# Four column tiles of 32 in place of two of 64, in the paired panels of a graph layer

## What is computed

```python
h = relu(layernorm(x))
u = par_u[0] * par_u[1] * (diag_u[:, None] * h[:2048] @ W_u) + h[:2048]
i = par_i[0] * par_i[1] * (diag_i[:, None] * h[2048:] @ W_i) + h[2048:]
e = concatenate([u, i])
h2 = adj @ (adj.T @ e)
out = x + layernorm(h2) * ln_gamma + ln_beta + h
```

## Time and profile before

| | us |
|---|---|
| median of 3 runs | 376.25 |
| lowest and highest | 376.2, 376.77 |
| span of the profiled execution | 374.4 |
| PE busy | 367.1 |
| DVE busy | 251.5 |
| ACT busy | 73.5 |
| POOL busy | 23.7 |

### The profile page before, as it was taken

One profiled execution on the slowest core, in us unless ns is written; L12 is line 12 of the kernel. 1 busy time (PEld: TensorE's weight loads), 2 busy tenths in 40 slices (PEclk: granted clock), 3 DMA queues, 4 the chain that ended last, 5 costly groups with the idle time before them and its releaser, 6 DMA issues.

```text
span 374.4 us, 8614 instructions
## 1 busy us (share of the span) xinstructions
PE 367.1 (98%) x3768; PEld 152.5 (41%) x3768; DVE 251.5 (67%) x249; ACT 73.5 (20%) x214; POOL 23.7 (6%) x30
## 2 busy tenths in 40 slices
PE   7999999999999999999999999999999999999995
PEld 5764455543334333433333343334333335436432
DVE  5999995859344965595289349754963793382366
ACT  4863012100032004000400320031004002202322
POOL 2023060000000000000000000000000000000036
PEclk9999999999999999999999999999999999999998
DMA  8999999999999999799969987997999699929603
GB/s 310 421 417 414 422 421 420 422 418 361 417 424 421 353 417 424 273 358 414 426 269 360 429 364 258 398 429 279 356 428 424 256 354 345 425 95 399 270 0 141
DMA packets 19896, 133.22 MB, mean 356 GB/s; under 512 B 2208, under 2 KB 2976, under 8 KB 4000
## 3 DMA queue, kind: packets, MB, share of 16 engines
q1 hardware_dynamic: 19440, 132.22, 87.4%
q10 hardware_dynamic: 432, 0.66, 0.5%
HBM read 131.55 MB, written 1.31 MB: 355 GB/s over the span
## 4 chain that ended last, share of the span: by engine, by line
PE 87%; DMA 7%; POOL 2%; SPq 2%; DVE 1%; issue 0%; ACT 0%; DVEq 0%; POOLq 0%
PE h_acc L756 35%; PE t_acc L782 32%; PE t_acc L725 10%; PE h_acc L739 9%; DMA natural<-adj_rows 7%; SPq L239 1%; POOL xs L360 1%; POOL scaled L356 1%; PE t_acc L800 1%; DVE xs L663 0%; SPq L236 0%; DVE scaled L652 0%; DVE natural L639 0%; PE h_acc L819 0%; DVE var L493 0%
## 5 line engine op out<-in xcount | busy, mean ns | idle before, releaser
L530 DVE STREAM_TRANSPOSE strips<-natural 128x2048 f32<-128x2048 f32 x76 | 168.2, 2274 | 48.4 <-PE h_acc L756 48.4
L756 PE MATMUL h_acc<-strips,centred 32*64 32x512 f32 x2432 | 133.3, 589 | 0.0
L782 PE MATMUL t_acc<-natural,e 128*64 128x512 f32 x560 | 121.4, 592 | 0.0
L756 PEld LDWEIGHTS h_acc<-strips,centred 32*64 32x64 f32 x2432 | 52.8, 132 | 78.5 <-issue 78.5
L782 PEld LDWEIGHTS t_acc<-natural,e 128*64 128x64 f32 x560 | 40.2, 137 | 79.9 <-issue 79.9
L725 PE MATMUL t_acc<-natural,e 128*64 128x256 f32 x480 | 54.1, 381 | 0.7 <-DMA natural<-adj_rows 0.6
L403 ACT COPY t_high<-t_acc 64x256 f32<-64x256 f32 x20 | 7.4, 368 | 212.6 <-PE t_acc L782 173.2
L539 DVE TENSOR_TENSOR t_sum<-t_acc,t_high 64x256 f32<-64x256 f32 x20 | 8.2, 410 | 57.0 <-ACT t_high L403 57.0
L725 PEld LDWEIGHTS t_acc<-natural,e 128*64 128x64 f32 x480 | 33.8, 137 | 20.6 <-issue 3.0
L410 ACT COPY centred<-centred 32x384 f32<-32x384 f32 (+2 forms) x60 | 24.2, 403 | 66.2 <-DVE centred L552 65.7
L739 PE MATMUL h_acc<-cols,centred 128*64 128x512 f32 x160 | 37.1, 599 | 0.0
(11 more groups left out here) (55 smaller groups left out, 86.6 us busy)
## 6 DMA issues: line engine op xcount, KB each, us to landing
natural<-adj_rows SPq DMA_DIRECT2D x100, 1024.0 KB, 11.8
cols<-adj_cols SPq DMA_DIRECT2D x20, 1024.0 KB, 7.6
natural<-adj_last SPq DMA_DIRECT2D x4, 1024.0 KB, 11.2
out<-xs SPq DMA_DIRECT2D x4, 256.0 KB, 2.0
xs<-x ACTq DMA_DIRECT2D x2, 256.0 KB, 5.4
xs<-x SPq DMA_DIRECT2D x2, 256.0 KB, 8.3
out<-xs SPq DMA_DIRECT2D x2, 128.0 KB, 2.0
smalls<-small SPq DMA_DIRECT2D x1, 150.0 KB, 3.3
```

The lines of the kernel that those rows point to most:

```text
L530: nc.vector.transpose(strips[:, a, :, m].rearrange("p c t i -> p t c i"), natural[:, a, m].rearrange("p t (c j) -> p t c j", j=Q)).then_in ...
L756: last = nc.tensor.matmul(h_acc[D * s:D * (s + 1), q], t[part, a, b, u, :], rows, start=(isinstance(g, int) and g == 0 and b == 0 and u == 0),
L782: last = nc.tensor.matmul(t_acc[D * s:D * (s + 1), c].rearrange("p (a w) -> p a w", a=2), e[:, GT * m + 2 * k + s, :], natural[:, :, m, HA ...
```

## The change

In `first_pair` each matmul of 64 stationary columns becomes two of 32, into PSUM partitions 0, 32, 64 and 96. The moving operand of the two with the same s is the same. `second_pair` calls a new function for the loaded columns that does the same there. Strips, single panels, the loaded columns of single panels, transfers and the work of the other engines stay as they are.

```diff
                     for k in range(HALF):
-                        for s in range(2):
-                            last = nc.tensor.matmul(t_acc[D * s:D * (s + 1), c].rearrange("p (a w) -> p a w", a=2),
-                                                    e[:, GT * m + 2 * k + s, :], natural[:, :, m, HALF * s + k],
+                        for s, v in itertools.product(range(2), range(D // Q)):
+                            lane = D * s + Q * v
+                            last = nc.tensor.matmul(t_acc[lane:lane + Q, c].rearrange("p (a w) -> p a w", a=2),
+                                                    e[:, GT * m + 2 * k + s, Q * v:Q * (v + 1)],
+                                                    natural[:, :, m, HALF * s + k],
                                                     start=(m == 0 and k == 0),
                                                     stop=(m == GROUPS - 1 and k == HALF - 1))
                     last.then_inc(s_first, 2)
+
+            def second_loaded_quarters(g, a, half):
+
+                pe.wait_ge(s_cols[a], 16 * (half + 1))
+                pe.wait_ge(s_t, g + 1)
+                for b in range(BLOCKS):
+                    for s, v in itertools.product(range(2), range(D // Q)):
+                        lane = D * s + Q * v
+                        last = nc.tensor.matmul(h_acc[lane:lane + Q, LOADED], t[:, a, b, 0, Q * v:Q * (v + 1)],
+                                                cols[:, a, s, b], start=False, stop=False, skip_group_check=True)
+                last.then_inc(s_loaded_done, 1)
 
             def second_pair(g, half):
                 for a in range(2):
                     second_strips(g + a, a).then_inc(s_strips_done, 1)
                 for a in range(2):
-                    second_loaded(g + a, a, half)
+                    second_loaded_quarters(g + a, a, half)
```

## The result

| | before | after |
|---|---|---|
| median of the runs, us | 376.23 | 399.81 |
| lowest and highest | 376.11, 376.77 | 399.61, 401.4 |
| ratio | | 1.0626 (1.0604 to 1.0647) |
| span of the profiled execution | 374.4 | 397.7 |

The direction and the place were foreseen, the size was not: 23.6 us where 4.9 was forecast, and the time lies above the range (376.3 to 388.0).

What follows compares the result with a forecast made beforehand. PE was taken to bound the kernel alone, any wait of PE adding in full. Borders with stagger +0.5 us and two jumps back +4.4 us on 376.25 gave 381.1 us, range 376.3 to 388.0.

Steps and rivals of the forecast that it cites:

- The rounds: Product 1 and loaded columns of the pairs: 336 rounds before and after, four column tiles running together, cost 0.
- Weight loads: They double in number, but four lie well inside a 0.43 us round, hidden by running matmuls.
- The borders: Three new ones where 128 x 32 meets 128 x 64, 0.15 us each; with the stagger +0.5 us (0 to 0.7).
- The stagger: Two further tiles add 13 ns at a round's start, paid at 14 borders at most where four-tile stages end: 0.2 us.
- That the loop's code no longer fits: PE's loop grows from 5.4 to 6.9 packets, one more ahead; code is refetched at the jumps back, chance 0.56.
- The price of a jump: Each of two jumps back waits for one packet: 4.7 - 2.5 = 2.2 us, together 4.4 us (0 to 11.0).
- The fetch: One instruction packet at a jump back takes 4.7 us, between bounds of 2.0 and 7.6.
- the lead of the sequencer: At the branch 20 to 29 matmuls are still queued on PE, hiding 2.5 us of the fetch (2.1 to 3.1).
- Later packets of the turn are asked for ahead and stay hidden.: After a jump back, only the first packet makes PE wait; later ones come as in the first turn, without cost.
- The wait is simply added.: While PE stands still at a jump, transfers and DVE go on, so nothing is late behind it.
- That the code still fits: Rival for PE's loop: jumps cost nothing, only +0.5 us remains, 376.7 us (376.25 to 377.0); chance 0.32.
- that four tiles don't run together: Rival for the rounds: they take twice their time, 520 us, or loads lose their cover, 423 us; chance 0.09.

Runs made afterwards that it cites:

- the moved loop of 1757 instructions: Changed kernel with four column tiles in product 1 only (loaded columns keep two), plus 52 waits (26 instructions) ahead of the loop: 378.42 us, ratio 1.0056.
- of 1501 instructions: Changed kernel with four column tiles in the loaded columns of the pairs only, product 1 keeping two of 64: 377.32 us, ratio 1.0022.
- the moved one: Whole change with 52 waits (26 instructions) ahead of the loop, so its first instruction begins a block of code: 389.4 us, ratio 1.0365.

## Why the prediction failed in size

**The rounds** were right. Four column tiles run together: product 1 is 160 matmuls in 17.17 us, to the hundredth what 80 took before. Nothing was won and nothing lost.

**Weight loads** were right: with twice as many of them product 1 takes the same 17.17 us, so they stay hidden.

**The borders** were right. Forecast +0.5 (0 to 0.7), measured 0.35 in the pairs. The price of a border where only the width changes, which no row of before showed, is 0.15 us (17.32 less 17.17), as taken; the three new ones are 0.14 (24.17 less 24.03), 0.15 (7.06 less 6.91) and 0.15 (10.51 less 10.36). The stagger, put at up to 0.2 us, didn't show: the loaded columns take 3.57 us where they took 3.58. That the loaded columns are quartered along with product 1 saves seven such borders, which the kernel with four tiles in product 1 only shows (17.30).

**That the loop's code no longer fits** was right, and the trace of before had left it open. The loop with two tiles of 64 and the same number of instructions loses the same, and the written-out loop loses 0.35 us in the pairs. The Trainium skill ("Runtime: NRT & Kernel Launch", section "Instruction fetch mechanics") has PE's store hold 2,048 instructions in blocks of 256, which makes eight of them. Every loop that ran agrees with this: cut into such blocks, the loops that touch seven and have one more ahead fit, those that touch eight or nine don't. No run here counts the blocks of the store directly; the packets of a turn are the nearest to it.

That the forecast came out on this side was in part luck. Its own count, 6.9 packets and one ahead, is what the moved loop of 1757 instructions has (1757 / 256 = 6.9), and that loop fits. The changed loop doesn't because it is longer than the 1792 counted, by the 29 instructions that are neither matmuls nor loads, and because of where it begins: it touches nine blocks.

**The price of a jump** is the step that failed, in three terms.

- The fetch. I put 4.7 us from `cols` in the second turn. The branch took 6.0 and 6.3 us. The lead of the sequencer was right: 2.5 us forecast, and PE had work until 174.45 us (178.22 less the wait of 3.77) when the branch came at 171.8, a lead of 2.65. So PE's first wait was 3.8 and 4.1 us in place of 2.2. The upper bound, 7.6, would have held this. Why the fetch takes 6 us stays open: the DMA engines were busy all through both waits (share 0.97 to 1.04 in the windows of the first jump), and no run has a jump with idle queues.
- "Later packets of the turn are asked for ahead and stay hidden." They were not, for the first of them: 3.53 us more, behind a few matmuls. I had worked out how long the loop is and not where it begins in its block. Moving it showed what this was worth: two waits a jump cost 22.83 / 2 = 11.4 us with what follows them, one costs 5.9 (the mean of 6.0 and 5.7).
- "The wait is simply added." It isn't: after the wait the granted clock was 0.50, and matmuls ran at a lower pace until it rose again. Behind the first jump the matmuls themselves took 1.93 + 8.62 = 10.55 us where 6.87 is usual, 3.7 us more, and behind the second 4.4 us more; with one wait it was 1.9 us.

For the first jump the terms add up: 3.77 and 3.53 us of waiting and 3.7 of slower matmuls are the 11.0 us that it cost (192.30 - 164.15 less 17.17). For the second 4.12, 3.32 and 4.4 make 11.8, and the two together the 22.8. The range was too narrow since its upper end held a bad value for the first term only, and neither of the other two was in any of its cases.

**The rivals.** That the code still fits came true only for other loops, of 1501 instructions and, moved by 26, of 1757. That four tiles don't run together was refuted by the pace.

## What to carry to other kernels

Splitting matmuls in two inside a loop doubles their instructions, and when the loop's code outgrows what the engine holds, every jump back pays, here 11.4 us: look in the trace for instruction packets from the second turn on, and at the branch's own duration, before and after. Where a long loop makes few turns, write it out, or shift it by a few instructions: here that was worth 10 to 23 us, with no work changed. And a wait of some 4 us on PE cost more than its length at all jumps looked at here, as the granted clock fell during it or just behind it.

## What the hardware showed that I had not expected

- The cost of a jump depends on the place of its target: 26 idle instructions ahead of a loop moved the time from 401.0 to 378.4 us.
- Once one block was gone, all of them were: the second and the third turn brought 10 packets each, not one. The code seems to be dropped in the order in which it came, so that each fetched block pushes out the next that is needed.
- Four column tiles of 128 x 32, two on the same moving data, run at the pace of two of 128 x 64 and of eight of 32 x 64: one round in 0.43 us.
- The granted clock fell to 0.50 around stands of PE of some 4 us: during the stand in the changed kernel, and only after PE had started again in the moved one. In one execution of the written-out kernel it fell in the opening stage, where PE had been busy for 4.78 of the 7.6 us before, and stayed there for 3.3 us of uninterrupted work.
